# Folded key sums, early exponentials, reordered splits and transfers, and both halves of a norm scaled before their low parts, in a two-layer cross-attention kernel

## The reference, cut to what matters

```
x = x + alpha * (softmax(x wq0' (ctx wk0')' / sqrt(512)) (ctx wv0')) wo0'          # one head
for l in (1, 2):                                                                   # 16 heads, K = 128
    h = layer_norm(x, scale_l, offset_l)
    q = h wq_l + bq_l
    keys, values = ctx wk_l + bk_l, ctx wv_l + bv_l, each with one more row, bias_k_l and bias_v_l
    x = x + softmax(q keys' / sqrt(128)) values wo_l + bo_l
x = x + gelu(layer_norm(x) w1 + b1) w2 + b2
```

## Time and profile before

| | us |
|---|---|
| median of three launches | 1841.67 |
| the profiled execution | 1845.13 |
| its span | 1843.3 |
| busy in it: TensorE | 1814.3 |
| busy: VectorE | 1119.8 |
| busy: ScalarE | 806.2 |
| busy: GpSimd | 773.3 |

### The profile page before, as it was taken

One profiled execution on the slowest core, in us unless ns is written; L12 is line 12 of the kernel. 1 busy time (PEld: TensorE's weight loads), 2 busy tenths in 40 slices (PEclk: granted clock), 3 DMA queues, 4 the chain that ended last, 5 costly groups with the idle time before them and its releaser, 6 DMA issues.

```text
span 1843.3 us, 30698 instructions
## 1 busy us (share of the span) xinstructions
PE 1814.3 (98%) x11548; PEld 1777.6 (96%) x11548; DVE 1119.8 (61%) x2518; ACT 806.2 (44%) x1868; POOL 773.3 (42%) x634
## 2 busy tenths in 40 slices
PE   8889999999999999999999999999999999999999
PEld 5789999999999999999999999999999999999999
DVE  3676556555575565566688555556666566555565
ACT  3534344434444434344475443444435334434354
POOL 2685252453162352531378245343245252353244
PEclk9999999999999999999999999999999999999999
DMA  8952011111020121210372112121112021111132
GB/s 249 241 172 63 29 53 41 47 58 41 12 76 24 47 59 34 64 31 29 109 227 85 39 47 58 30 58 41 30 52 59 24 62 31 47 58 41 35 100 85
DMA packets 73590, 123.80 MB, mean 67 GB/s; under 512 B 13888, under 2 KB 25536, under 8 KB 73444
## 3 DMA queue, kind: packets, MB, share of 16 engines
q1 hardware_dynamic: 71140, 117.64, 21.8%
q10 hardware_dynamic: 2304, 4.20, 0.7%
HBM read 119.20 MB, written 2.61 MB: 66 GB/s over the span
## 4 chain that ended last, share of the span: by engine, by line
PE 89%; DVE 5%; DMA 2%; ACT 2%; SPq 1%; issue 1%; DVEq 0%; ACTq 0%
PE psum L589 27%; PE psum L590 27%; PE psum L591 27%; PE psum L875 4%; DMA ctxT_in<-ctxT_dram 1%; DVE xT L1536 1%; DMA ctx_rows_in<-ctx_dram 1%; PE psum L750 1%; PE psum L841 1%; DVE h_lo L1342 1%; PE psum L602 1%; PE psum L598 1%; DVE psum L1504 1%; PE psum L599 0%; PE psum L768 0%
## 5 line engine op out<-in xcount | busy, mean ns | idle before, releaser
L471 POOL TENSOR_TENSOR wbuf_hi<-stage,zero_col 128x512 fp32r<-128x512 f32 x256 | 267.5, 1045 | 916.1 <-PE psum L591 545.2
L521 POOL TENSOR_TENSOR wbuf_lo<-stage,wbuf_hi 128x512 fp32r<-128x512 f32 x256 | 329.5, 1287 | 20.1
L589 PE MATMUL psum<-pT_hi,ctx_rows_hi 121*128 121x250 f32 (+3 forms) x1152 | 332.0, 288 | 1.2 <-DVE pT_lo L1338 1.2
L591 PE MATMUL psum<-pT_hi,ctx_rows_lo 121*128 121x250 f32 (+3 forms) x1152 | 332.3, 288 | 0.0
L590 PE MATMUL psum<-pT_lo,ctx_rows_hi 121*128 121x250 f32 (+3 forms) x1152 | 331.1, 287 | 0.0
L589 PE MATMUL psum<-ctxT_hi,a_hi 128*125 128x362 f32 (+1 forms) x832 | 280.5, 337 | 0.0
L1338 DVE TENSOR_TENSOR a_lo<-psum,a_hi 128x500 fp32r<-128x500 f32 (+2 forms) x288 | 146.2, 526 | 210.2 <-ACT a_hi L996 209.5
L591 PE MATMUL psum<-ctxT_hi,a_lo 128*125 128x362 f32 (+1 forms) x832 | 273.2, 328 | 0.0
L590 PE MATMUL psum<-ctxT_lo,a_hi 128*125 128x362 f32 (+1 forms) x832 | 272.9, 328 | 0.0
L589 PE MATMUL psum<-a_hi,wbuf_hi 128*128 128x400 f32 x720 | 254.0, 353 | 0.0
L590 PE MATMUL psum<-a_lo,wbuf_hi 128*128 128x400 f32 x720 | 248.4, 345 | 0.0
(11 more groups left out here) (183 smaller groups left out, 3563.8 us busy)
## 6 DMA issues: line engine op xcount, KB each, us to landing
stage<-head_w_dram SPq DMA_DIRECT2D x256, 256.0 KB, 2.6
mlp_stage<-mlp_w_dram SPq DMA_DIRECT2D x32, 512.0 KB, 3.9
ctx_rows_in<-ctx_dram SPq DMA_DIRECT2D x12, 726.0 KB
ctxT_in<-ctxT_dram SPq DMA_DIRECT2D x12, 724.0 KB, 10.3
key_stage<-head_w_dram SPq DMA_DIRECT2D x32, 256.0 KB, 7.4
l0w<-l_w_dram ACTq DMA_DIRECT2D x16, 256.0 KB, 8.4
kb<-diff_scratch SPq DMA_DIRECT2D x32, 64.0 KB, 4.3
out_dram<-y_out SPq DMA_DIRECT2D x8, 200.0 KB, 2.6
```

The lines of the kernel that those rows point to most:

```text
L471: return nc.gpsimd.tensor_tensor(out, in_, zero_col[0:in_.shape[0], :].broadcast_to(tuple(in_.shape)), ALU.add)
L521: nc.gpsimd.tensor_tensor(lo, held, hi.bitcast(F32), ALU.subtract).then_inc(stage_free, 1)
L589: pe.matmul(out, a_h, x_hi, start=start, stop=False)
L591: return pe.matmul(out, a_l, x_hi, start=False, stop=stop)
```

## The change

1. **Key sums.** GpSimd's multiplication and the `kw` tiles are gone. VectorE makes a key's sum from the loaded tiles with four multiply-and-sum instructions over 128x128, each followed in the built program by an instruction that reads out the accumulator (128x1).
2. **Where the keys lie.** Twenty-one keys (`KEYS_BEFORE`) are summed in the single head, four of them loaded as soon as the difference rows are in DRAM, which SyncE's queue now waits for ahead of the second half's context. The other eleven go one by one through one pair of tiles (`key_stage_late`, `kb_late`) and are summed at places of the first layer's steps ("a" ahead of the second block's maximum, "b" after the step's pieces); their loads stand behind given weight loads, and each waits for the sum before it. No key stands inside the norm; `key_parts(0)` stands there, `key_parts(1)` goes to step (3, 2).
3. **Early exponentials** and the order of context splits in the single head on ScalarE and VectorE.
4. **Norms.** VectorE inverts and scales both halves, then makes the low parts of both. TensorE runs the high-part products of both halves, interleaved over the three (in the MLP two) outputs, then the low-part products.
5. GpSimd may begin with the first two weight matrices at once; the third waits for the 21 keys.

```
-KEYS = 7
+KEYS, EARLY_KEYS, KEY_WBUF = 7, 4, 2
+LATE_KEYS_AT = {
+    (0, 0): "b", (0, 1): "ab", (0, 2): "ab", (0, 3): "ab", (1, 0): "b", (1, 1): "b", (1, 2): "b", (1, 3): "b",
+}
+LATE_KEYS_BEHIND = {8: 1, 12: 1, 14: 2, 15: 5, 17: 1, 21: 1}
...
             sp.wait_ge(diff_out, 16)
+            sp.wait_ge(dv_out, 32)
+            some_key_weights(EARLY_KEYS)
             for b in range(3):
                 sp.wait_ge(ls_mm, b + 1)
-                if b == 0:
-                    some_key_weights(4)
                 load_ctx_columns(1, b)
...
+                    sp.wait_ge(kw_sum, i)
+                    sp.dma_start(kb_late[:, :], diff_d[i].partition_broadcast(P)).then_inc(late_ld, 16)
+                    sp.dma_start(key_stage_late[:, :], head_w_d[i * 4 + KINDS.index("q")]).then_inc(late_ld, 16)
...
+                        if ph == 0:
+                            some_key_weights(LATE_KEYS_BEHIND.get(i, 0))
...
+            def products_of_norm(j, outs, highs, lows):
+                for n in range(2):
+                    for c in range(DC):
+                        pe.wait_ge(n_hi, n_chunks(j, n, c))
+                        for out, a_h, a_l in zip(outs, highs, lows):
+                            pe.matmul(out[:, piece(n)], a_h(c), h_hi[:, c, piece(n)], start=(n == c == 0), stop=False)
+                            pe.matmul(out[:, piece(n)], a_l(c), h_hi[:, c, piece(n)], start=False, stop=False)
+                for n in range(2):
+                    for c in range(DC):
+                        pe.wait_ge(n_lo, n_chunks(j, n, c))
+                        ends = [pe.matmul(out[:, piece(n)], a_h(c), h_lo[:, c, piece(n)], start=False,
...
                 if j == BETWEEN:
                     pe.wait_ge(m_add, (half * FB - 1) * DC + 1)
...
+                exp0(0)
                 ctx_columns_hi(0, 3)
+                exp0(1)
                 ctx_rows_hi(0, 2)
-                exp0(0)
+                probs0_hi(0)
                 x1_hi_parts()
-                probs0_hi(0)
-                exp0(1)
                 exp0(2)
...
             def key_sums(i):
-                dve.wait_ge(kw_s, i + 1)
-                nc.vector.tensor_reduce(w0[:, :, i], kw[i % len(kw)][:, :, :], AX_X, ALU.add).then_inc(kw_sum, 1)
...
+                for c in range(DC):
+                    summed = nc.vector.tensor_tensor_reduce(
+                        out=chunk(held, c), in0=chunk(held, c), in1=diffs[:, :], scale=1.0, scalar=0.0, op0=ALU.mult,
+                        op1=ALU.add, accum_out=w0[:, c, i:i + 1])
+                summed.then_inc(kw_sum, 1)
...
                 for n in range(2):
                     norm_invert(j, n)
                     norm_scale(j, n)
-                    norm_lo(j, n)
+                norm_lo(j, 0)
+                norm_lo(j, 1)
...
-                        if ph == 0 and before is None:
-                            key_parts(1)
                         run_pieces((k, b, "a"))
+                        if ph == 0 and "a" in LATE_KEYS_AT.get((k, b), ""):
+                            some_key_sums(1)
                         maxima(k, b, 1)
```

More of the change, by code:

```diff
@@ L182, in build @@
                 prob0 = sb("prob0", [P, 2, T], F32, batches)
-                kb = [sb(f"kb{j}", [P, P], F32, batches) for j in range(3)]
+                kb = [sb(f"kb{j}", [P, P], F32, batches) for j in range(EARLY_KEYS, KEYS)]
             sb("l0w_space", [P, 4 * DC * D], F32, single)
@@ L192, in build @@
                 dv_hi, dv_lo = split("dv", [LAYERS * H, P], bias_rows)
[L193 to L195 removed]
+            kb_first = [sb(f"kb{j}", [P, P], F32, single) for j in range(EARLY_KEYS)]
+            key_stage = [sb(f"key_stage{j}", [P, D], F32, single) for j in range(EARLY_KEYS)]
         with ExitStack() as mlp:
@@ L551, in _ @@
                             pool.wait_ge(n_lo, n_chunks(BETWEEN, 0, DC - 1))
+                        if ph == 0 and i == KEY_WBUF:
+                            pool.wait_ge(kw_sum, max(k for k in range(KEYS_BEFORE) if k % KEYS >= EARLY_KEYS) + 1)
                         if ph == 0 and i == WBUFS - 1:
-                            pool.wait_ge(kw_sum, LAYERS * H)
+                            pool.wait_ge(kw_sum, KEYS_BEFORE)
                             pool.wait_ge(dv_out, 32)
@@ L591, in mm3 @@
                 return pe.matmul(out, a_l, x_hi, start=False, stop=stop)
-            def product_of_norm(out, a_h, a_l, j, n):
-                for c in range(DC):
-                    pe.wait_ge(n_hi, n_chunks(j, n, c))
-                    pe.matmul(out, a_h(c), h_hi[:, c, piece(n)], start=(c == 0), stop=False)
-                    pe.matmul(out, a_l(c), h_hi[:, c, piece(n)], start=False, stop=False)
-                for c in range(DC):
-                    pe.wait_ge(n_lo, n_chunks(j, n, c))
-                    mm = pe.matmul(out, a_h(c), h_lo[:, c, piece(n)], start=False, stop=(c == DC - 1))
-                return mm
+            def products_of_norm(j, outs, highs, lows):
[9 more added lines that the diff above has]
+                        ends = [pe.matmul(out[:, piece(n)], a_h(c), h_lo[:, c, piece(n)], start=False,
+                                          stop=(n == 1 and c == DC - 1)) for out, a_h in zip(outs, highs)]
+                return ends
             def product(out, a_h, a_l, x_hi, x_lo):
@@ L892, in attend @@
                             mm.then_inc(u_mm, 1)
-                for n in range(2):
-                    first_queries(0, n)
-                    bias_scores(n)
-                    first_queries(1, n)
+                first_products()
                 if j == BETWEEN:
@@ L969, in hidden @@
                         .then_inc(g_mm, 1)
-                for n in range(2):
-                    for fb in range(2):
-                        first_hidden(fb, n)
+                first_hidden()
                 for fb in range(FB):
@@ L1523, in norm_dve @@
                 if j == 0:
-                    some_key_sums(4)
+                    key_parts(0)
                 for n in range(2):
@@ L1682, in layer @@
                             normalise(k, b, 2)
+                    if ph == 0:
+                        some_key_sums("b" in LATE_KEYS_AT.get((k, b), ""))
+                        if (k, b) == (3, 2):
+                            key_parts(1)
                     before = k, b
```

129 lines of the change are left out of this document (61 added, 68 removed).

## The result

| | us |
|---|---|
| changed kernel, median of 6 executions | 1853.43 (1852.88 to 1861.14) |
| kernel before, median of 6 beside them | 1840.95 (1839.01 to 1846.27) |
| ratio, 95% interval | 1.0077 [1.0058, 1.0096] |
| profiled execution of the changed kernel; its span | 1853.81; 1852.0 |

The change makes the kernel 12.5 us slower; I had forecast no change (1840.5 us), in a range that ended at 1852. With the later comparisons the kernel before has medians of 1839.5 to 1840.7 us, so its profiled execution (1845.13) lies some 5 us above what it mostly takes, and the two profiles differ by only 8.7 us.

What follows compares the result with a forecast made beforehand. TensorE, busy 98%, was taken as the bound, with recoverable idle time and low clock ahead of 200 us. Terms -9.6 + 0.7 - 2.0 + 5.4 + 2.4 + 2.0 = -1.1 gave 1844.0, against the median 1840.5 us; range 1829 to 1852.

Steps and rivals of the forecast that it cites:

- Single head, -2.0: Single head: up to 7.7 us gained, against later context and VectorE's dearer keys handing over the residual late; net -2.0 us.
- The gain of up to 7.7 us: Single head: exponential waits (3.1 us), low clock behind them (up to 3.5) and a low-part wait (1.1) go.
- Later context, +1.5: Single head: second half's context lands about 2 us later, ScalarE stands before it once, costing TensorE some 1.5 us.
- Layer 1 to its first attended block, -9.6 + 0.7: First sum of layer 1's norm to turning at (0, 1): causes of delay go, -9.6 us; bare norm split +0.7.
- Late keys, +5.4: Layer 1's steps: eleven keys wait on SyncE's loads and delay TensorE, +5.4 us in sum, between 0 and 10.
- The 1.7 at the turning of (0, 3): Layer 1: the late key following that of step (0, 1), summed at 189.1 us, makes this turning 1.7 us late.
- the 1.2 behind it: Layer 1: the two late keys after the one delaying the turning of (0, 3) cost 1.2 us together.
- Norms, +2.4: Norms of layers and MLPs: bare splits cost more than the new order saves; +2.4 us, between 0 and +5.
- Clock, +2.0: Whole kernel: the clock falls behind some of the new waits of 1.4 to 2.5 us; +2.0 us, 0 to 8.
- Rival B: Single head: VectorE becomes the bound if a key takes 2.2 us or more, residual 10 us later; 1853.5 us, chance 0.10.
- B's sign: From 85 to 120 us: VectorE near full and the norm's sums waiting for the residual by more than 3 us.

Runs made afterwards that it cites:

- no_late: Changed kernel without the eleven late keys, loads and sums (a small memset in place of each): 1850.3 us.
- norms_only: Kernel before with only the change's new norm order: 1846.8 us, ratio to before 1.0031.
- no_lock: Changed kernel where GpSimd clears the low parts of the second set of context rows instead of subtracting; all 21 key sums stay: 1844.9 us.
- sums_behind: Changed kernel with no key sum between the fourth block's low part and the seventh's, the other 17 behind it; transfers as in the change: 1848.1 us.
- early_exp: Kernel before with only the new order of exponentials and context splits in the single head: 1840.9 us, ratio to before 1.0004.
- late_ahead: Changed kernel with one late key's load ahead of the load of matrix 14 instead of behind it: 1850.9 us.
- the two swaps: Norm order of before put into the changed kernel, 1849.5 us; new norm order put into the kernel before, 1846.8 us.
- keys_behind: Changed kernel with 17 key sums moved behind the seventh block's low part, and second-half context columns and rows issued ahead of most keys: 1847.4 us.

## Why the prediction was wrong

**Single head, -2.0: the step that failed.** I took every key at one price, 1.4 us, which is VectorE's work alone, and left the lock out of the sum, though I had the rule and one sign of it (`ctxT_lo` at 2.35 us in place of 1.5). The bare key is cheaper than I took, 0.85 us; the locked ones take 1.5 to 5.2 in the profile after, and 8.2 in `no_late`. Where they stand decides, since three of the four in the profile after are in front of a maximum. Against the start that `norms_only` shows, the single head gives not -2.0 but +7.9 us; `no_lock` gives 8.5 back at the median, and `sums_behind` all of it in its profile. The Trainium skill, SBUF — State Buffer, "Who interferes with whom", says that a VectorE instruction with two SBUF inputs contends with a GpSimd one that reads SBUF, not with one that only writes it, over a lock that is exclusive. The traces agree: the rows shown end with GpSimd's subtraction, and beside its clearing a key instruction keeps its 0.28 us. I had sized it at 2 to 4 us of VectorE's time and should have asked what waits behind each locked instruction.

**The gain of up to 7.7 us in that step** was read from an execution that took 3.5 us more than the median. The low clock after 51 us is not in the profile of `norms_only`, where the same code reaches the norm 4.6 us sooner; I had subtracted the 3.5 us between profile and median at the end and counted the same low clock as a gain before. `early_exp` measured nothing.

**Later context, +1.5.** There in the profile after, by the path that I had named: the last rows came at 94.88 us, ScalarE stood in front of them, and TensorE waited 2.17 us, or 3.9 with the low clock. But the later transfers are not shown to be its reason. `early_exp` has two such waits (1.56 and 1.22 us) with the old transfers, and `sums_behind` none with the new ones; `norms_only`, with ScalarE's old order, has none either. So the wait goes with the early exponentials and with the moment when rows land, which is 89.1 to 94.9 us in seven profiles of the same transfers. I had booked the new order as a pure gain.

**Layer 1 to its first attended block, -9.6 + 0.7.** Right: from 123.86 to 159.23 us it takes 35.4 us; I had said 35. Without the late keys (`no_late`) the whole layer takes 388.3 us, 8.2 less than before; I had said 8.9.

**Late keys, +5.4.** Right in place and size at `attend` of (0, 1): 2.78 us, said 2.5, by the load I had named. The 1.7 at the turning of (0, 3) and the 1.2 behind it are 0.15 us together. The first wait doesn't hide them: in `late_ahead`, where it is gone, they are 0.2 us, so I had them too large. Another, 1.38 us for a residual at 242 us, was not in my list. With the low clock it is 6.6 us in the profile. (The key that I had at 189.1 us comes out at 188.5 by the terms that I gave.)

**Norms, +2.4.** The waits were right one by one (a_lo 1.33, said 1.45; y_out 1.93, said 1.9), the sum too small: 3.9 and 6.1 us by the two swaps. The term that was too small is the second layer: +1.2 and +1.5 us where I had 0.7 each, since I had set 0.9 us against the bare split for products that no longer wait for low parts. The last MLP gave +0.1 where I had -0.2; its bare split is 1.8 us.

**Clock, +2.0.** In the profile after, five spells of 3.4 us at 1.2 GHz cost 8.5 us, each behind a wait of 1.78 us or more; not every such wait has one behind it, as `norms_only` shows. The profiled execution before had as much (17 us at the low level), and most other executions of it less, by their mean clock (0.998 against 0.995).

**Rival B** came nearest: VectorE's keys make the residual late, 1853.5 us. The number is luck: its mechanism was wrong. A key of 2.2 us of work was its condition; `no_lock` does all the work and has the norm 9.3 us sooner. The norm's sums did not wait for the residual either, which was B's sign. The Trainium skill, Vector Engine (DVE) Microarchitecture Reference, "Points that are easy to get wrong", has half throughput for the form `S2S2D2_STT` with two non-bf16 SBUF sources, the rule that I had named with B. Whether this instruction is of that form no run shows, and it did not run at half throughput: 128 columns at the 1.03 ns of a one-input instruction and the 0.08 us of a read-out are the 0.21 us measured.

## What to carry to other kernels

Before work is moved from GpSimd to VectorE as instructions with two SBUF inputs, lay them beside GpSimd's rows: beside a subtraction or copy of GpSimd between SBUF tiles such an instruction took up to 3.6 us in place of 0.28, and a chain of short ones can wait once for each of GpSimd's. Put them where nothing urgent stands behind them, or keep the form with one input. And take gains from an execution near the median, not from one above it: a low-clock spell in the profile may be gone already.

## What the hardware showed that I had not expected

One key of four instructions waited for three of GpSimd's in turn (3.56, 3.49 and 1.11 us), and in that execution the start was longer than the change's (127.0 against 123.9 us) although its context rows had landed sooner. The subtraction of GpSimd held these instructions up, its MEMSET of the same tile did not (0.28 us in the middle of one, `no_lock`). A CAST of 128x64 with one input was held up by a MEMSET all the same: 1.97 us beside one and 0.19 us without; in `keys_behind` it took 2.08. The multiply-and-sum instruction takes 0.21 us from start to start for 128 columns, its read-out in it.
